# Twelve ident-by-xnT products at the head of TensorE's expert tile loop, each behind a wait on a scatter count

## The chip, the cores and the metric

The kernel runs on one core of a Trainium2 chip. The metric is the device time in microseconds (us) of one execution; lower is better. Three runs of the kernel before gave 1662.21, 1662.52 and 1665.05 us.

## What is computed

A chain of eight layers over an input `x` of 2048 tokens by 128 features, all in float32, each added to `x` (`x = x + layer(layernorm(x))`): a Mamba layer, a first mixture of experts, a linear attention, a second (gated) mixture of experts, then attention, experts, attention and a feed-forward layer. The change touches the function that computes the two mixtures of experts. In the reference they are:

```
# first: 8 experts, the best two of each token, 128 -> 512 -> 128
def body(acc, p):
    w1e, b1e, w2e, b2e, ce = p
    h = jax.nn.relu(xf @ w1e + b1e)
    y = h @ w2e + b2e
    return (acc + y * ce[:, None], None)
# second: the same with a gate
    h = jax.nn.silu(xf @ wg) * (xf @ wu)
    acc = acc + w[:, None] * (h @ wd)
```

`ce` and `w` are zero for all but a token's two best experts.

## The kernel before, in words

`program` calls one function per layer; `experts` is called twice, for `moe0` (not gated) and `moe1` (gated). Every function writes its work in one or more `nc.Block()` groups. In a block each engine has a list of its own: TensorE (PE), VectorE (DVE), ScalarE (ACT), GpSimd (POOL) and SyncE (SP, which only starts DMAs). Inside a block the engines meet only through semaphores that the code names.

`experts` computes only the pairs of token and expert that are chosen, in tiles of 128 rows (P = 128). It has two blocks:

- **The routing block** (line 903). The engines normalise `x` (16 tiles of 128 tokens, T = 16, in C = 4 chunks of CW = 512 tokens), turn it into `xnT`, compute the router's logits, pick two experts per token, and count for every pair a slot in a DRAM table `slots`, where each expert has a region of its own. POOL then sends the rows there: line 921 starts 2T = 32 indirect DMAs of 128 rows each, the **scatters**, and each adds 16 to the semaphore `s_sent` when it has landed. In `moe0` PE and DVE also add the second bias, beside the first scatters (lines 960 to 1060).
- **The tile block** (line 1087). NT = 2T + E - 1 = 39 tiles are computed one after the other (E = 8). SP waits until `s_sent` is 16 x 32, reads the first row of 13 tiles from the table `basei` (line 1083, a register load), and loads tile after tile from `slots` into 12 buffers `xg` (line 1095). PE reads the experts of 13 tiles from `whoi` (line 1083 too) and then runs a pipeline with four steps per tile: `turn_x` transposes the tile (line 1121), `hidden` multiplies by the expert's first matrix (line 1128; in `moe1` by a second one too, line 1131), `turn_h` transposes the result (line 1138), `down` multiplies by the last matrix (line 1147). DVE and ACT take the results out of the PSUM banks (lines 1175, 1192, 1199, 1202, 1208), and POOL sends the tile's answers out with an indirect DMA (line 1111). The register loads of PE and SP come again before tiles 13 and 26.

The weights `wa`, `wu`, `ba`, `wd` are loaded by DMAs of the routing block; their semaphore is `s_w`. `bank[7]` is a PSUM bank that `turn_h` uses for tiles of odd number. `k.ident` is a 128x128 identity and `k.xnT` the turned input, both float32.

The lines that the change and the prediction touch stand in TensorE's list of the tile block:

```
                pe.wait_ge(s_w, 16 * len(weights))
                for i in range(-2, NT + 1):
                    if 0 <= i + 2 < NT:
                        if (i + 2) % GROUP == 0:
                            experts_of.update(enumerate(values(ENGINE.PE, whoi, i + 2, E - 1), i + 2))
                        turn_x(i + 2)
```

Of the kernel before, what the change touches and what calls it, by code (L numbers as in the profile page):

```python
# [34 lines left out]
CW = CT * P  # L35
# [6 lines left out]
class Core:  # L42
# [64 lines left out]
    def sem(self, name):  # L107
        handle = self.nc.alloc_semaphore(name=name)
        self.part_sems.append(handle)
        return handle  # L110
# [726 lines left out]
def experts(k, name, gated):  # L837


    nc, t, C, T, E = k.nc, k.t, k.C, k.T, k.E  # L840
    L0, bank, pre = k.L, k.bank, name
# [2 lines left out]
    ROW = k.ROW  # L844
    NT = 2 * T + E - 1
    NB, NY, GROUP = 12, 6, 13
    slots, answers = k.slots[name], k.answers[name]
    tmp = ExitStack()
    sb = lambda n, shape, dt=F32: k.sb(f"{name}_{n}", shape, dt, tmp)
    sem = lambda n: k.sem(f"{name}_{n}")  # L850
    with tmp:
# [37 lines left out]
        s_w, s_v, s_rank, s_rows, s_same, s_slot, s_table, s_sent = (  # L889
            sem(n) for n in ("weights", "routing", "rank", "rows", "same_rows", "slot", "table", "sent"))  # L890
# [12 lines left out]
        with nc.Block() as block:  # L903
            @block.sync
            def _(sp):
                for dst, src in gates:
                    sp.dma_start(dst, src).then_inc(g_w, 16)
                for dst, src in weights:
                    sp.dma_start(dst, src).then_inc(s_w, 16)
# [158 lines left out]
        def wait(engine, sem, count):  # L1068

            if count > 0:  # L1070
                engine.wait_ge(sem, count)

        def loaded(engine, i):
            engine.wait_ge(s_ld[i % NB], 16 * (i // NB + 1))
# [5 lines left out]
        def values(engine, table, i, top_value):  # L1080

            reason = "counted up to the number of tiles, and the expert is held below their number"
            return nc.values_load_multi_w_load_instructions(
                table[0:1, i:min(i + GROUP, NT)], engines=[engine], min_val=0, max_val=top_value,
                skip_runtime_bounds_check_because=reason)[1]

        with nc.Block() as block:
# [26 lines left out]
            @block.tensor  # L1114
            def _(pe):
                experts_of = {}

                def turn_x(i):
                    loaded(pe, i)
                    wait(pe, s_xT, i)  # L1120
                    nc.tensor.transpose(bank[0][:, 0:P], xg[:, i % NB, 0:P], k.ident[:]).then_inc(s_tx, 1)  # L1121

                def hidden(i):
                    pe.wait_ge(s_xT, i + 1)
                    wait(pe, s_sg if gated else s_hh, i - 1)
                    one = bass.ds(experts_of[i], 1)
                    flat = lambda w: w[:, one, :].rearrange("p o f -> p (o f)")
                    nc.tensor.matmul(bank[1 + i % 2][:], xgT[:, i % 2, :], flat(wa), start=True, stop=True).then_inc(s_g, 1)  # L1128
                    if gated:
                        wait(pe, s_hh, i - 1)  # L1130
                        nc.tensor.matmul(bank[3 + i % 2][:], xgT[:, i % 2, :], flat(wu), start=True, stop=True)\
                            .then_inc(s_u, 1)

                def turn_h(i):
                    pe.wait_ge(s_hh, i + 1)
                    wait(pe, s_hT, i - 1)
                    for f in range(FB):
                        last = nc.tensor.transpose(bank[5 + 2 * (i % 2)][:, f * P:(f + 1) * P],  # L1138
                                                   h[:, i % 2, f * P:(f + 1) * P], k.ident[:])
                    last.then_inc(s_th, 1)  # L1140

                def down(i):
                    pe.wait_ge(s_hT, i + 1)
                    wait(pe, s_yw, i)
                    one = bass.ds(experts_of[i], 1)
                    for f in range(FB):
                        last = nc.tensor.matmul(bank[6][:, 0:P], hT[:, i % 2, f, :],  # L1147
                                                wd[:, one, f, :].rearrange("p o d -> p (o d)"),
                                                start=(f == 0), stop=(f == FB - 1))
                    last.then_inc(s_y, 1)  # L1150

                pe.wait_ge(s_w, 16 * len(weights))
                for i in range(-2, NT + 1):
                    if 0 <= i + 2 < NT:
                        if (i + 2) % GROUP == 0:
                            experts_of.update(enumerate(values(ENGINE.PE, whoi, i + 2, E - 1), i + 2))
                        turn_x(i + 2)
                    if 0 <= i + 1 < NT:
                        hidden(i + 1)
                    if 0 <= i < NT:  # L1160
                        turn_h(i)
                    if 0 <= i - 1:
                        down(i - 1)
# [1410 lines left out]
def program(nc, t, out, parts=PARTS):  # L2574
    with ExitStack() as ctx:
        k = Core(nc, ctx, t)
        for part in parts:
            if part == "mamba":
                mamba(k)
            elif part in ("moe0", "moe1"):  # L2580
                experts(k, part, gated=(part == "moe1"))
            elif part == "linear":
                linear(k)
            elif part in ("decay", "window"):
                softmax_mixer(k, part, windowed=(part == "window"))
            elif part == "deep":
                deep(k)
            elif part == "ffn3":
                ffn3(k)
            k.end_part()  # L2590
        store(k, out)
# [64 lines left out]
```

## Time and profile before

| what | value |
|---|---|
| three runs | 1662.21, 1662.52, 1665.05 us |
| the profiled execution | 1660.62 us |
| its span (first to last instruction) | 1658.8 us |
| mean granted TensorE clock, as a share of full speed | 0.864 |
| PE busy | 1204.5 us (73%) |
| DVE busy | 875.2 us (53%) |
| ACT busy | 651.1 us (39%) |
| POOL busy | 532.7 us (32%) |
| scatters (line 921) | 64, from 447.3 us to 732.3 us |

The profiled execution took 1660.62 us, 1.8 us more than its span; the sums of the prediction are made against it. The tile block of `moe0` lies at about 490 to 600 us of the span, that of `moe1` at about 736 to 880 us. A float32 matmul of 512 columns leaves two MATMUL records in the trace. The granted clock stands at 0.50 or 1.00, 1.2 or 2.4 GHz. "PEq", "SPq" and so on are an engine's sequencer: semaphores, branches, register loads, DMA issues.

### The profile page before, as it was taken

To read this page: it belongs to the slowest core of one execution; us is meant where nothing else is said; L and a number is where in the kernel's file an instruction comes from. 1 tells how busy PE (TensorE), PEld (TensorE's weight loads), DVE (VectorE), ACT (ScalarE), POOL (GpSimd) and SP (SyncE) were. 2 spreads that over 40 slices of the span, in tenths; PEclk is the share of its full clock that TensorE was granted. 3 is DMA by queue.
4 is the path that set the end of the run, shared out by engine and by line. 5 is a ranking of instruction groups with operands and counts; after the bars stand their busy time and mean duration, and the time that the engine had idled before them with its cause. 6 is when DMAs were issued, how large, how long until landed. Compare 5 with 4: busy or idle time off the path is not lost. (4 is left out here: it accounts for less than half of the span.)

```text
span 1658.8 us, 23925 instructions
## 1 busy us (share of the span) xinstructions
PE 1204.5 (73%) x8267; PEld 723.8 (44%) x8267; DVE 875.2 (53%) x2052; ACT 651.1 (39%) x1106; POOL 532.7 (32%) x661
## 2 busy tenths in 40 slices
PE   6605776768339948219991799988982799969998
PEld 3201222225327735206660577763331567744544
DVE  3407999995515452503336688854653667651010
ACT  2605555553102210103330677745652676632131
POOL 6107765662253320352234322202007544300000
PEclk9858999999559975559995799998995999979999
DMA  2993000000411120511102000001000000020000
GB/s 64 189 188 60 1 0 1 0 0 1 162 55 53 48 69 1 167 56 36 42 28 67 2 2 2 3 2 39 1 1 8 1 3 2 2 72 1 0 0 25
DMA packets 88024, 60.26 MB, mean 36 GB/s; under 512 B 15346, under 2 KB 78724, under 8 KB 87780
## 3 DMA queue, kind: packets, MB, share of 16 engines
q1 hardware_dynamic: 83364, 49.38, 14.0%
q0 software_dynamic: 4544, 9.38, 1.7%
q8 instruction: 68, 1.11, 0.3%
q14 instruction: 48, 0.39, 0.1%
HBM read 30.21 MB, written 28.52 MB: 35 GB/s over the span
## 5 line engine op out<-in xcount | busy, mean ns | idle before, releaser
L809 POOL TENSOR_TENSOR hC<-h,Cs 128x1024 f32<-128x1024 f32 x64 | 153.3, 2395 | 137.4 <-DVE h L738 137.1
L599 PE MATMUL bank<-hC,ident 128*128 128x512 f32 x256 | 129.2, 628 | 43.8 <-POOL hC L809 43.7
L738 DVE TENSOR_TENSOR_SCAN h<-bank,state,dBx 128x512 f32<-128x512 f32 x128 | 157.2, 1270 | 2.2 <-ACT bank L674 0.2
L1111 POOL DMA_INDIRECT moe_answers<-moe_yw,moe_xg x78 | 74.7, 958 | 173.6 <-DVE moe_yw L1208 173.6
L2057 DVE TENSOR_REDUCE window_mx<-bank 128x2 f32<-128x384 f32 x128 | 69.6, 556 | 76.1 <-PE bank L1912 75.0
L1175 ACT ACTIVATE moe_hT<-bank 128x512 f32<-128x512 f32 x78 | 46.6, 597 | 154.8 <-PE bank L1138 154.8
L727 DVE TENSOR_TENSOR dBx<-dtx,bank 128x1024 f32<-128x1024 f32 x64 | 76.6, 1196 | 49.0 <-PE bank L586 49.0
L2057 DVE TENSOR_REDUCE decay_mx<-bank 128x2 f32<-128x512 f32 x128 | 85.1, 685 | 25.0 <-PE bank L1912 24.8
L674 ACT ACTIVATE bank<-dt,A 128x512 f32<-128x512 f32 x128 | 83.2, 682 | 37.9 <-DVE h L738 37.9
L2027 ACT ACTIVATE decay_pb<-bank 128x512 f32<-128x512 f32 x128 | 75.6, 596 | 48.0 <-PE bank L1925 45.5
L599 PEld LDWEIGHTS bank<-hC,ident 128*128 128x128 f32 x256 | 44.4, 192 | 106.7 <-POOL hC L809 71.1
L586 PE MATMUL bank<-BC,sel 128*128 128x512 bf16 x64 | 25.5, 398 | 87.4 <-PEq L258 57.6
L178 ACT ACTIVATE xnT<-bank 128x512 f32<-128x512 f32 x24 | 14.3, 597 | 179.6 <-PE bank L169 179.6
L1147 PE MATMUL bank<-moe_wd,moe_hT 128*128 x624 | 83.1, 276 | 1.9 <-DVE moe_yw L1208 1.9
L1128 PE MATMUL bank<-moe_wa,moe_xgT 128*128 x156 | 84.4, 623 | 0.0
L1121 PE MATMUL bank<-ident,moe_xg 128*128 128x128 f32 x78 | 22.5, 288 | 82.5 <-DMA moe_xg<-moe_slots 74.6
L921 POOL DMA_INDIRECT moe_slots<-moe_rows,moe_slot x64 | 61.7, 963 | 59.8 <-DVE moe_slot L1014 40.9
L158 POOL TENSOR_TENSOR rstd<-veps,mhalf 128x4 f32<-128x4 f32 (+1 forms) x14 | 23.3, 1664 | 172.3 <-DVE veps L140 172.0
L1147 PEld LDWEIGHTS bank<-moe_wd,moe_hT 128*128 128x128 f32 x624 | 76.3, 193 | 2.6 <-issue 2.6
L2027 ACT ACTIVATE window_pb<-bank 128x384 f32<-128x384 f32 x128 | 61.6, 487 | 40.0 <-PE bank L1925 39.7
L680 ACT ACTIVATE Cs<-bank 128x512 f32<-128x512 f32 x64 | 38.2, 596 | 73.7 <-POOL hC L809 65.3
L169 PE MATMUL bank<-ident,xn 128*128 128x128 f32 x64 | 17.2, 424 | 68.3 <-DVE xn L149 68.3
(452 smaller groups left out, 2912.9 us busy)
## 6 DMA issues: line engine op xcount, KB each, us to landing
moe_slots<-blank SPq DMA_DIRECT2D x16, 1040.0 KB, 17.9
moe_xg<-moe_slots SPq DMA_DIRECT2D x78, 65.0 KB, 1.8
moe_wa<-in_moe_w SPq DMA_DIRECT2D x2, 2048.0 KB, 9.3
moe_back<-moe_answers SPq DMA_DIRECT2D x16, 256.0 KB, 4.8
moe_ba<-in_moe_b SPq DMA_DIRECT2D x1, 2048.0 KB, 14.2
moe_wu<-in_moe_wu SPq DMA_DIRECT2D x1, 2048.0 KB, 14.3
deep_w<-in_deep_w SPq DMA_DIRECT2D x3, 512.0 KB, 5.0
moe_answers<-moe_yw,moe_xg POOLq DMA_INDIRECT x78, 2.2
```

Source lines behind the costliest of these rows:

```text
L599: last = nc.tensor.matmul(sum_bank(hh)[:], k.ident[:], hC[:, u % 2, hh, :], start=(n == 0), stop=(n == NS - 1))
L674: nc.scalar.activation(decay_bank(u, hh)[:], dt[:, hh, cols(c)], ACT.Exp, scale=A[:, hh, n:n + 1]).then_inc(q_dA, 1)
L727: v.tensor_tensor(dBx[:, u % 2], dtx[:, :, cols(c)], b_bank[:, None, :].to_broadcast([P, H, CW]), ALU.mult).then_inc(q_dBx, 1)
L738: v.tensor_tensor_scan(h[:, u % 2, hh, :], decay_bank(u, hh)[:], dBx[:, u % 2, hh, :], state[:, n, hh:hh + 1], ALU.mult, ALU.add).then_inc ...
L809: g.tensor_tensor(hC[:, u % 2], h[:, u % 2], Cs[:, u % 2, None, :].to_broadcast([P, H, CW]), ALU.mult).then_inc(q_hC, 1)
L921: nc.gpsimd.indirect_dma_start(slots, bass.IndirectOffsetOnAxis(index, 0), rows[j][:, i, :], None)\
L1111: nc.gpsimd.indirect_dma_start(answers, bass.IndirectOffsetOnAxis(index, 0), yw[:, i % NY, :], None)\
L1128: nc.tensor.matmul(bank[1 + i % 2][:], xgT[:, i % 2, :], flat(wa), start=True, stop=True).then_inc(s_g, 1)
L1147: last = nc.tensor.matmul(bank[6][:, 0:P], hT[:, i % 2, f, :], wd[:, one, f, :].rearrange("p o d -> p (o d)"), start=(f == 0), stop=(f == ...
L1175: nc.scalar.activation(hT[:, i % 2].rearrange("p f q -> p (f q)"), bank[5 + 2 * (i % 2)][:], ACT.Copy if gated else ACT.Relu).then_inc(s_h ...
L2027: nc.scalar.activation(pb[:, w % 4, :], bank[2 + w % 2][:, 0:2 * HW], ACT.Exp).then_inc(s_ex, 1)
L2057: nc.vector.tensor_reduce(mx[:, 2 * g:2 * g + 2], bank[g % 2][:, 0:2 * HW].rearrange("p (j q) -> p j q", j=2), AX.X, ALU.max, negate=True) ...
```

## The change

At the head of TensorE's list in the tile block, behind the wait for the weights and ahead of the first register load, a loop of twelve steps is added. Each step waits until `s_sent` has reached the count of 20, 21, ... 31 scatters, and then makes one product of `ident` with the first 512 columns of `xnT` into `bank[7]`. Nothing reads the result.

```
@@ experts @@
     NB, NY, GROUP = 12, 6, 13
+    BUSY = 12
     slots, answers = k.slots[name], k.answers[name]
@@ tile block, TensorE @@
                 pe.wait_ge(s_w, 16 * len(weights))
+                for sent in range(2 * T - BUSY, 2 * T):
+                    pe.wait_ge(s_sent, 16 * sent)
+                    nc.tensor.matmul(bank[7][:], k.ident[:], k.xnT[:, 0:CW], start=True, stop=True)
                 for i in range(-2, NT + 1):
```

Below stand TensorE's instructions in program order around the border of the two blocks of `moe0`. Line numbers of the changed kernel are one higher up to the loop and four higher behind it. Semaphores are named in such rows by the first that held their number: `m_sel` is `s_sent` here, `w_in` is `s_w`, `m_rstd` the load of the first tile; the barrier is named in full. Before:

```order
L967 MATMUL bank<-moe_bd,moe_combT 128x128 x3
L903 UNCONDITIONAL_BRANCH
L1114 UNCONDITIONAL_BRANCH [waits barrier_Pool_Activation_PE_DVE_SP_release]
L1083 TENSOR_LOAD moe_whoi [waits w_in]
L1121 MATMUL bank<-ident,moe_xg 128x128 [waits m_rstd]
L1121 MATMUL bank<-ident,moe_xg 128x128 [waits m_dt_relu,m_xn]
```

And in the changed kernel:

```order
L968 MATMUL bank<-moe_bd,moe_combT 128x128 x3
L904 UNCONDITIONAL_BRANCH
L1115 UNCONDITIONAL_BRANCH [waits barrier_Pool_Activation_PE_DVE_SP_release]
L1156 MATMUL bank<-xnT,ident 128x512 [waits m_sel,w_in]
L1156 MATMUL bank<-xnT,ident 128x512 [waits m_sel] x11
L1084 TENSOR_LOAD moe_whoi
L1122 MATMUL bank<-ident,moe_xg 128x128 [waits m_rstd]
```

The twelve products stand between the branch into the tile block and the register load; `moe1` has the same rows. The list of POOL, in the changed kernel, at the same border:

```order
L158 TENSOR_TENSOR rstd<-veps,mhalf 128x12 [waits ln_ve]
L922 DMA moe_slots<-moe_rows,moe_slot 17408x130 [waits c_ident,c_more,c_zeroed,filled]
L922 DMA moe_slots<-moe_rows,moe_slot 17408x130 x31
L904 UNCONDITIONAL_BRANCH
L1107 UNCONDITIONAL_BRANCH [waits barrier_Pool_Activation_PE_DVE_SP_gather]
```

All 32 scatters stand ahead of POOL's branch at the block's end, as before; POOL gathers the barrier that releases the other engines. No instruction of POOL, DVE, ACT or SP has moved.

## Rows read from the trace of the kernel before

**Rows 1.** The page: busy time of each engine, its share, instructions.
```profile
PE 1204.5 (73%) x8267; PEld 723.8 (44%) x8267; DVE 875.2 (53%) x2052; ACT 651.1 (39%) x1106; POOL 532.7 (32%) x661
```
**Rows 2.** Waits of TensorE, 430 to 500 and 680 to 745: total, times, longest.
```profile
PE bank L1121 <- DMA moe_xg<-moe_slots: 25.6, 1, 25.6
...
PE bank L1121 <- DMA moe_xg<-moe_slots: 49.0, 1, 49.0
```
**Rows 3.** Instructions of line 921: ns min/median/max, first and last start; time to landing.
```profile
L921 POOL DMA_INDIRECT moe_slots<-moe_rows,moe_slot x64: 954/958/1220, 447.3 to 732.3; - x64
...
DMA to landing us min/median/max: 2.3/2.3/3.4
```
**Rows 4.** Sequencer instructions of line 903, the routing block's end, same columns.
```profile
L903 POOLq EVENT_SEMAPHORE  x4: 17/17/17, 490.4 to 736.1; - x4
...
L903 PEldq DRAIN  x2: 575/1336/2098, 466.4 to 689.8; - x2
...
L903 POOLq DRAIN  x2: 17805/17815/17825, 472.5 to 718.1; - x2
...
L903 PEldq EVENT_SEMAPHORE  x2: 51/51/51, 490.5 to 736.1; - x2
```
**Rows 5.** PE's register loads of line 1083, 485 to 500 and 730 to 745.
```profile
L1083 PEldq TENSOR_LOAD <-moe_whoi x1: 1307/1307/1307, 490.6 to 490.6; - x1
...
L1083 PEldq TENSOR_LOAD <-moe_whoi x1: 1096/1096/1096, 736.3 to 736.3; - x1
```
**Rows 6.** Timeline, both tile blocks' first instructions: start, us, engine, line.
```profile
494.00 0.48 PE L1121 MATMUL bank<-ident,moe_xg 128*128 128x128 f32 x1 [25.57 <-DMA moe_xg<-moe_slots]
...
739.41 0.47 PE L1121 MATMUL bank<-ident,moe_xg 128*128 128x128 f32 x1 [49.05 <-DMA moe_xg<-moe_slots]
...
740.67 1.95 PE L1128 MATMUL bank<-moe_wa,moe_xgT 128*128 x2
742.41 1.92 PE L1131 MATMUL bank<-moe_wu,moe_xgT 128*128 x2
...
747.01 1.02 PE L1128 MATMUL bank<-moe_wa,moe_xgT 128*128 x2
747.87 0.59 PE L1131 MATMUL bank<-moe_wu,moe_xgT 128*128 x1
```
**Rows 7.** Windows: stretch, length, busy of PE, PEld, DVE, ACT, POOL, granted clock, DMA, GB/s.
```profile
494.00:499.40 5.40, 4.92 (x10) 2.35 (x11) 1.66 (x5) 0.00 (x0) 0.00 (x0) 0.50 0.50 120
499.40:505.00 5.60, 5.60 (x36) 4.15 (x35) 3.34 (x8) 1.79 (x3) 0.96 (x1) 1.00 0.06 18
739.40:745.15 5.75, 5.20 (x8) 2.28 (x9) 1.37 (x4) 0.60 (x1) 0.00 (x0) 0.50 0.51 121
...
1494.80:1499.50 4.70, 4.70 (x6) 2.12 (x7) 0.53 (x1) 1.97 (x2) 0.00 (x0) 0.50 0.00 0
```
**Rows 8.** Instructions of line 599, whose operands have the added product's shape and type.
```profile
L599 PE MATMUL bank<-hC,ident x256: 590/592/1223, 138.8 to 381.6; 128*128 128x512 f32 x128
```
**Rows 9.** PE's register load before tile 26 of `moe0`, and the timeline beside it.
```profile
L1083 PEldq TENSOR_LOAD <-moe_whoi x1: 3210/3210/3210, 553.9 to 553.9; - x1
...
554.04 1.06 PE L1147 MATMUL bank<-moe_wd,moe_hT 128*128 x8
...
557.28 0.33 PE L1121 MATMUL bank<-ident,moe_xg 128*128 128x128 f32 x1 [2.18 <-issue]
```
**Rows 10.** Windows, same columns: behind that load, and after the last tile of `moe0`.
```profile
557.40:560.80 3.40, 3.40 (x10) 2.15 (x10) 0.98 (x2) 0.33 (x1) 0.00 (x0) 0.50 0.14 34
...
595.00:598.40 3.40, 0.07 (x1) 0.00 (x0) 0.35 (x1) 0.00 (x0) 0.96 (x1) 1.00 0.13 41
598.40:600.00 1.60, 0.00 (x0) 0.00 (x0) 0.00 (x0) 0.00 (x0) 0.00 (x0) 0.50 0.31 84
```
**Rows 11.** Windows, same columns: a long stretch of the tile block of `moe1`.
```profile
747.00:860.00 113.00, 110.36 (x589) 74.63 (x588) 43.28 (x105) 41.81 (x70) 32.58 (x34) 1.00 0.13 36
```
**Rows 12.** Instructions of line 586, 512 columns in bf16, one record each.
```profile
L586 PE MATMUL bank<-BC,sel x64: 379/389/609, 131.8 to 371.7; 128*128 128x512 bf16 x64
```

More of the change, by code:

```diff
@@ L846, in experts @@
     NB, NY, GROUP = 12, 6, 13
+    BUSY = 12
     slots, answers = k.slots[name], k.answers[name]
@@ L1152, in _ @@
                 pe.wait_ge(s_w, 16 * len(weights))
+                for sent in range(2 * T - BUSY, 2 * T):
+                    pe.wait_ge(s_sent, 16 * sent)
+                    nc.tensor.matmul(bank[7][:], k.ident[:], k.xnT[:, 0:CW], start=True, stop=True)
                 for i in range(-2, NT + 1):
```

## The prediction

> **What bounds the kernel now.** The page comes first: TensorE is the busiest engine, with 73% of the span [rows 1]. A share over eight layers says little of one place, so the reading goes to the place that is edited. The waits of TensorE around it come next: two are long, 25.6 and 49.0 us, both of line 1121, and both end with a load from the slot table [rows 2]. They are the time in which POOL starts the scatters. So at the head of each tile block TensorE has nothing to do until the first tile has come; behind that it is the bound: in `moe1` it is busy for 110.36 of 113.00 us [rows 11]. Whatever holds TensorE beyond the arrival of the first tile moves the whole tile block, and with it everything behind it, by as much.
>
> The windows show the second fact. When the first tile comes (494.0 and 739.4 us), the granted clock is 0.50, the lower of its levels; it stays there for 5.40 and 5.75 us and is 1.00 afterwards [rows 7]. In these stretches TensorE is busy for 4.92 and 5.20 us. At twice the clock this work takes half as long, so a TensorE that is at 2.4 GHz when the first tile arrives saves at most 2.46 + 2.60 = 5.1 us in the two parts. That is all that there is to be gained.
>
> The third view decides: what stands between the scatters and TensorE's list of the tile block. The new products are in the tile block, the scatters in the routing block. The program order shows a barrier there that POOL gathers and that releases the others. In the trace, TensorE's drain at the end of the routing block starts at 466.4 and 689.8 us, long before the scatters are out, but its semaphore instruction behind it comes only at 490.5 and 736.1 us [rows 4]. POOL's own drain starts at 472.5 and 718.1 us and takes 17.8 us: it ends at 490.3 and 735.9 us, and POOL's semaphore instructions follow at 490.4 and 736.1. The last scatter starts at 732.3 us and lands 2.3 us later by the median, 3.4 at most [rows 3]: at 734.6 to 735.7 us, before the barrier opens. **So TensorE can't be beside a scatter with anything that stands in the tile block.** When it gets there, all 32 have landed, the twelve waits on `s_sent` hold nothing back, and the twelve products run in one piece.
>
> **The change part by part.** Removed: nothing. Moved: TensorE's first register load, from the head of the block to behind the products. Added in each of the two parts: twelve waits and twelve float32 products of 512 columns.
>
> *The waits.* 0 us, since their counts are reached. If they weren't, they would be the thing wanted.
>
> *The products, start.* Before, the register load of TensorE is its first instruction in the block and starts at 490.6 and 736.3 us [rows 5]. The products take that place. With about 0.2 us to the first of them, they start at 490.8 and 736.5 us.
>
> *The products, length.* At the low clock two products of this size follow each other 742.41 - 740.67 = 1.74 us apart, at the high one 747.87 - 747.01 = 0.86 us [rows 6]. Those have another stationary operand than the identity; the one group with the identity and 512 float32 columns has 592 ns for a record, as have theirs, and 1223 at most [rows 8]. I take the clock to rise after as long a stretch as it did for the work that now starts here, 5.40 and 5.75 us [rows 7]. In `moe0` 5.40 / 1.74 = 3.1 products are slow and 8.9 fast: 5.40 + 8.9 x 0.86 = 13.1 us. In `moe1` 5.75 / 1.74 = 3.3 are slow: 5.75 + 8.7 x 0.86 = 13.2 us. They end at 503.9 and 749.7 us.
>
> *The delay.* The first tile's transpose started at 494.00 and 739.41 us [rows 6]; now it starts at 503.9 and 749.7. That is 9.9 + 10.3 = 20.2 us later, on the engine that bounds the block. The loads of SP aren't delayed: twelve tiles lie ready.
>
> *The clock.* TensorE comes to the first tile at the high clock and gets back the 2.46 + 2.60 = 5.1 us from above.
>
> *The register load.* It took 1.3 and 1.1 us at this place [rows 5] and is now behind the products. I cost it at nothing, and its cover is the products: before tile 26 the same load starts at 553.9 us, when the last eight records of line 1147 are only about to run (554.04, for 1.06 us) [rows 9]. So TensorE's sequencer runs ahead of its array by at least sixteen instructions with their weight loads, four of the new products and 3.4 us of time, more than either load. If it doesn't, the load adds 1.3 + 1.1 = 2.4 us, and if it takes the 3.2 us that it took there, 6.4 us.
>
> *What moves with the tile block.* The stalls of the later register loads fall at other moments. After the one before tile 26 the clock was low for 3.40 us [rows 10], which cost half of it, 1.7 us; after the other three it wasn't. With another phase it can be none of four, or two: -1.7 to +1.7 us. I take 0.
>
> The sum is 20.2 - 5.1 = **+15.1 us** against the profiled execution: a span of 1658.8 + 15.1 = 1673.9 us and a time of 1660.62 + 15.1 = 1675.7 us. The median of the three runs is 1.9 us above the profiled execution. The prediction is for the median: 1662.5 + 15.1 = **1677.6 us**, 0.9% slower.
>
> *A rule against the row.* Two neighbouring products of this shape stand 1.74 us apart at the low clock and 0.86 at the high one [rows 6]. The Trainium skill, in "TensorE: Matmul & The Clock Gate", section "Back-to-back issue gap", gives the gap as the number of columns over 1.2 GHz cold and over 2.4 GHz warm plus 2.5 ns, and makes no difference by type; by it twelve products would take 12 x 0.427 = 5.1 us, the end would be at 495.9 and 741.6, and the sum 4.1 - 5.1 = -1 us. The rows have four times that distance for float32, and I follow them.
>
> **The rivals.**
>
> *The products cost what bf16 products cost.* The nearest row is line 586, 512 columns in bf16, one record of 389 ns by the median and 609 at most [rows 12]. Twelve would be done in at most 12 x 0.61 = 7.3 us, at 498.1 and 743.8 us: 4.1 + 4.4 - 5.1 = +3.4 us, 1666 us. Against it: operand types are float32 in the diff, and line 599 with the same types has two records of 592 ns each. 2%.
>
> *It works as it is worded, and the kernel gets faster.* If TensorE entered the tile block while POOL was still at its scatters, the products would be spread over the last twelve, the last behind the 31st landing, at about 733.4 us. Even at 0.86 us it ends before the first tile arrives at 739.41. Nothing is late, and the gain is up to 5.1 us: 1657.4 us. It decides at one point: the first product must start before 736.1 us (490.5 in `moe0`). For it speaks only the semaphore that the loop waits for; against it TensorE's semaphore instruction at 490.5 and 736.1 behind a drain that was over at 468.5 and 690.4 [rows 4]. And then the gap of some 5 us to the first tile would count: after the last tile of `moe0` the clock is down 3.4 us into the idle time [rows 10], so that the first tile would find 1.2 GHz again and the time would be 1662.5. The same page of the Trainium skill, section "HAM oscillation — how this bites in real kernels", says this of bursts with waits for data between them, which speaks against the change even where it does what it says. 3% for both: 1% faster, 2% no change.
>
> *The register load isn't covered.* +2.4 to +6.4 us on top of the sum, 1680 to 1684 us. 10%.
>
> *The clock rises sooner or later.* If it rose at once, the twelve would take 12 x 0.86 = 10.3 us; if it never did, 12 x 1.74 = 20.9 us, and the 5.1 us would be lost too. The second isn't credible for a TensorE without a pause. Three starts lie between 4.70 and 5.75 us [rows 7], the first of them the last layer's, where TensorE is as dense as with the new products. 4.70 gives 12.7 us for the products. I allow twice the spread of the three, 2 us sooner or later, which is 1 us per part: -2 to +2 us. This is the width of the forecast and not a case of its own.
>
> **How the numbers follow.** Forecast 85%, load uncovered 10%, bf16 price 2%, as worded 3%. The range takes in the forecast's own width (2 us for the clock and 1.7 for the phases on each side: 1673.9 to 1681.3), a us below it for the start of the products, and the nearer end of the uncovered load: **1673 to 1682.5 us**. What lies outside are the two small rivals and the farther end of the load. A measurement of this kernel can tell about 0.2%, 3.3 us, from no change; the bf16 price, +3.4, sits on that bound and is counted within it. Faster 1%, within it 4%, slower 95%.
>
> **What would show it.** Right: in the changed kernel twelve products (24 records) of the new line in one piece from about 490.8 and 736.5 us, none before 490.5 or 736.1; the first three or so 1.7 us apart, the rest 0.86; the first transpose of line 1122 at 503 to 505 and 749 to 751 us, with no wait for a DMA, and at clock 1.00; TensorE's register load inside the stretch of the products; POOL's scatters and drain unchanged; every later layer's start some 15 us later. Wrong: products between 472 and 490 us, or spaced 1.26 us like the scatters; an idle TensorE of over 1 us between the last product and the first transpose; products of 0.4 us.

## The result and the profile after

| | before | changed |
|---|---|---|
| runs | 1662.12, 1662.21, 1662.52, 1665.05 us | 1672.54, 1674.94, 1675.11, 1675.12 us |
| median | 1662.37 us | 1675.03 us |
| profiled execution / span | 1660.62 / 1658.8 us | 1672.54 / 1670.7 us |

The changed kernel is slower: the ratio is 1.0069 with a 95% interval of 1.0051 to 1.0086, +12.7 us between the medians. The forecast was +15.1 us and 1677.6 us in a range of 1673 to 1682.5. On another chip, later in the study, the same two kernels stood at 1.0096 (1.0079 to 1.0112), +15.5 us between the medians.

The page, and the new line's instructions (ns min/median/max, first and last start), in the changed kernel:

```profile
span 1670.7 us, 24015 instructions
PE 1225.2 (73%) x8307; PEld 733.1 (44%) x8315; DVE 875.4 (52%) x2052; ACT 651.1 (39%) x1106; POOL 531.6 (32%) x661
...
L1156 PE MATMUL bank<-xnT,ident x48: 592/592/1193, 492.1 to 756.9; 128*128 128x512 f32 x48
```

TensorE has 20.7 us more busy time [rows 1], and its weight loads 9.3 us; VectorE, ScalarE and GpSimd are within 1.1 us of before. The 48 records are two for each of 24 products, none of them before 492.1 us. (Weight loads rose by 48, matmul records only by 40: eight matmul records are missing from this trace.)

The sequencers at the end of the routing block (line 904 now), and TensorE's first register load, same columns:

```profile
L904 PEldq DRAIN  x2: 573/1336/2100, 467.7 to 697.6; - x2
L904 POOLq DRAIN  x2: 17799/17823/17847, 473.8 to 725.9; - x2
...
L904 PEldq EVENT_SEMAPHORE  x2: 51/51/51, 491.9 to 743.8; - x2
...
L1084 PEldq TENSOR_LOAD <-moe_whoi x1: 1316/1316/1316, 497.3 to 497.3; - x1
```

As before [rows 4], TensorE drains early and is released at 491.9 and 743.8 us, when POOL's drain is over (473.8 + 17.8 = 491.6). The register load runs from 497.3 to 498.6 us, while the products run.

The timeline of TensorE (start, us, engine, line) at both tile blocks:

```profile
492.12 13.08 PE L1156 MATMUL bank<-xnT,ident 128*128 128x512 f32 x24 [22.36 <-PEq L904]
505.04 0.27 PE L1122 MATMUL bank<-ident,moe_xg 128*128 128x128 f32 x1
...
508.53 1.06 PE L1129 MATMUL bank<-moe_wa,moe_xgT 128*128 x2
...
744.10 13.38 PE L1156 MATMUL bank<-xnT,ident 128*128 128x512 f32 x24 [46.02 <-PEq L904]
757.32 0.27 PE L1122 MATMUL bank<-ident,moe_xg 128*128 128x128 f32 x1
...
762.45 1.02 PE L1129 MATMUL bank<-moe_wa,moe_xgT 128*128 x2
```

The twelve lie in one piece, 0.2 and 0.3 us behind the release, and the first transpose follows without a wait, where it had waited for a DMA [rows 6]. Windows (stretch, length, busy of PE, PEld, DVE, ACT, POOL, granted clock, DMA, GB/s):

```profile
492.10:497.20 5.10, 5.08 (x6) 2.18 (x7) 0.00 (x0) 0.00 (x0) 0.00 (x0) 0.50 0.31 73
497.20:505.00 7.80, 7.80 (x19) 3.37 (x18) 0.00 (x0) 0.00 (x0) 0.00 (x0) 1.00 0.22 56
744.10:749.80 5.70, 5.70 (x7) 2.49 (x8) 0.00 (x0) 1.10 (x1) 0.00 (x0) 0.50 0.31 73
749.80:757.30 7.50, 7.50 (x18) 3.18 (x17) 0.00 (x0) 0.00 (x0) 0.00 (x0) 1.00 0.21 53
```

So the slow stretch now holds three products and not the first tile [rows 7]; the first tile comes at 2.4 GHz.

A yardstick for the rest: from TensorE's release at the barrier to its first product of the third tile (line 1128), where the pipeline runs evenly. It holds the delay and the clock of one part and nothing of the other layers.

| kernel | `moe0`, us | `moe1`, us |
|---|---|---|
| before, first chip | 499.67 - 490.5 = 9.2 | 747.01 - 736.1 = 10.9 |
| changed | 508.53 - 491.9 = 16.6 | 762.45 - 743.8 = 18.7 |

Together +15.2 us, against a forecast of 15.1. The span grew by 11.9 only. Where each step now starts later: the release in `moe0` 1.4 us, its third tile 8.9, the load of its answers (line 1101) 10.5, the last products of the linear attention (line 1378) 7.7, the release in `moe1` 7.7, its third tile 15.4, the first product of the attention behind it (line 1871) 15.5, of the third expert layer (line 1503) 14.0, of the last layer (line 2496) 12.3, and the final store 11.9. The two steps of the change are in that ladder (+7.4 and +7.8, to the rounding); the other steps are 1.4 us lost ahead of them, 1.6 lost behind the third tile of `moe0`, and 2.8, 1.5 and 1.7 won in three later layers.

### The profile page after: what moved, and what is told of

It is laid out like the page before. It is cut to its first block and busy times, and to the rows that moved or that the text cites. A ratio compares the mean times of both kernels' runs of the same rounds, so it can differ in the third digit from the quotient of the medians.

```text
span 1670.7 us, 24015 instructions
## 1 busy us (share of the span) xinstructions
PE 1225.2 (73%) x8307; PEld 733.1 (44%) x8315; DVE 875.4 (52%) x2052; ACT 651.1 (39%) x1106; POOL 531.6 (32%) x661
## 5 line engine op out<-in xcount | busy, mean ns | idle before, releaser
L2061 DVE TENSOR_REDUCE decay_mx<-bank 128x2 f32<-128x512 f32 x128 | 85.2, 685 | 23.6 <-PE bank L1916 23.2
L1156 PE MATMUL bank<-xnT,ident 128*128 128x512 f32 x48 | 26.5, 718 | 68.4 <-PEq L904 68.4
L1196 DVE COPY moe_xgT<-bank 128x128 f32<-128x128 f32 x78 | 22.0, 283 | 95.7 <-PE bank L1122 95.4
```

The source lines that it names most:

```text
L2061: nc.vector.tensor_reduce(mx[:, 2 * g:2 * g + 2], bank[g % 2][:, 0:2 * HW].rearrange("p (j q) -> p j q", j=2), AX.X, ALU.max, negate=True) ...
```

## The experiments

They ran on three other chips (experiments 1 to 4 on one, 5, 7, 8 and the first run of 6 on the next, the rest on the last), so each is compared with the kernel before on its own chip (median 1656 to 1659 us there) by its ratio, and by the yardstick. No kernel leaves out a part of the computation; they differ in products that nothing reads. Twelve were run.

**1. The products without their waits.**

```
-                for sent in range(2 * T - BUSY, 2 * T):
-                    pe.wait_ge(s_sent, 16 * sent)
+                for _ in range(12):
```

> The changed kernel without its twelve waits on the scatter count; the twelve products stay at the head of the tile block. Theory (the barrier between the blocks holds TensorE until all scatters have landed, so the waits hold nothing back): same as the changed kernel, 1675 +- 1.5 us, first product 0.2 us behind TensorE's semaphore instruction at the barrier, products 13.1 and 13.4 us long. Rival (the waits themselves delay TensorE, or pace the products): at least 3 us faster than the changed kernel, with the products closer together.

Measured: ratio 1.0073 (1.0050 to 1.0096), as the changed kernel. Products 0.15 and 0.1 us behind the release, 13.49 and 12.47 us long; yardstick 17.0 and 17.7 us. The waits hold nothing back.

**2. The waits without the products.**

```
                 for sent in range(2 * T - BUSY, 2 * T):
                     pe.wait_ge(s_sent, 16 * sent)
-                    nc.tensor.matmul(bank[7][:], k.ident[:], k.xnT[:, 0:CW], start=True, stop=True)
```

> The changed kernel without its twelve products; the twelve waits stay. Theory (all of the loss is the time of the products): same as the kernel before, 1662.4 +- 1.5 us, first transposes 3.5 and 3.3 us behind the barrier as before. Rival (waits cost): each wait of some tenths of a us ahead of the register load makes the first transpose late, 1664 us and above.

Measured: 0.9996 (0.9983 to 1.0010). First transposes 3.3 and 3.2 us behind the release, yardstick 8.3 and 10.9 us. The waits cost nothing; all of the loss is the products.

**3. The products moved into the routing block.** The wait for `s_bx` is in `moe0` alone, where the bias adds read bank 7; `s_side` holds one semaphore for each of the scatters 20 to 31, which counts in place of `s_sent`.

```
                         last.then_inc(s_bo, 1)
+                    pe.wait_ge(s_bx, C)
+                for s in s_side:
+                    pe.wait_ge(s, 16)
+                    nc.tensor.matmul(bank[7][:], k.ident[:], k.xnT[:, 0:CW], start=True, stop=True)
@@ tile block, SyncE @@
-                sp.wait_ge(s_sent, 16 * 2 * T)
+                sp.wait_ge(s_sent, 16 * (2 * T - BUSY))
+                for s in s_side:
+                    sp.wait_ge(s, 16)
```

> The twelve products moved to the end of TensorE's list in the routing block, each behind a semaphore of its own of one of the scatters 20 to 31 (none at the head of the tile block). Theory (only there can they be beside scatters): the products lie between about 472 and 490 us, nothing is late, and nothing is added to the path. The clock rises about 5 us into them; whether it is still high at the first tile, 4 to 5 us after the last product, decides the gain: if it has fallen again 1662.4 us, if it holds until 494.0 and 739.4 us 1658 us (4.4 us less). I expect it to have fallen, 1662.4 +- 1.5 us. Rival (the place does not matter, the products cost their time wherever they stand): 1670 us and above.

Measured: 1.0082 (1.0064 to 1.0099), a miss for the whole. The two parts differ. TensorE in `moe1`, timeline:

```profile
732.23 8.60 PE L976 MATMUL bank<-xnT,ident 128*128 128x512 f32 x14 [29.37 <-DMA moe_slots<-moe_rows,moe_slot]
741.13 3.38 PE L976 MATMUL bank<-xnT,ident 128*128 128x512 f32 x6 [0.31 <-DMA moe_slots<-moe_rows,moe_slot]
744.77 2.29 PE L976 MATMUL bank<-xnT,ident 128*128 128x512 f32 x4 [0.26 <-DMA moe_slots<-moe_rows,moe_slot]
752.43 0.48 PE L1130 MATMUL bank<-ident,moe_xg 128*128 128x128 f32 x1 [5.38 <-DMA moe_xg<-moe_slots]
```

Here they do lie beside the scatters, paced by them once the clock is high, and the last ends at 747.1 us, 1.6 us before the release at 748.7. But the windows behind them:

```profile
747.00:750.60 3.60, 0.06 (x1) 0.00 (x0) 0.00 (x0) 1.28 (x1) 0.00 (x0) 1.00 0.00 0
750.60:757.40 6.80, 4.42 (x8) 1.99 (x9) 0.59 (x3) 0.60 (x1) 0.00 (x0) 0.50 0.48 110
```

The clock falls at 750.6 us, 3.5 us into the idle time, and the first tile meets 1.2 GHz again: yardstick 759.65 - 748.7 = 11.0 us, nothing gained. That is the "works as it is worded" rival in its case of no gain. In `moe0` the timelines of DVE and PE say:

```profile
489.79 0.69 DVE L1064 TENSOR_TENSOR X<-bank,X 128x512 f32<-128x512 f32 x1 [11.98 <-remote]
490.54 12.56 PE L976 MATMUL bank<-xnT,ident 128*128 128x512 f32 x24 [10.60 <-DVE X L1064]
```

VectorE's last bias add came late, the products waited for it because of bank 7, and their 12.6 us stood ahead of the barrier, which opened at 503.3 us. POOL's drain was over at 487.7 us, so the products held the barrier; the whole lost 12.5 us by the medians. The wait for the bank that I had added is the loss.

**4. The same with three more products at the head of the tile block.** The lines below are added to experiment 3.

```
                 pe.wait_ge(s_w, 16 * len(weights))
+                for _ in range(3):
+                    nc.tensor.matmul(bank[7][:], k.ident[:], k.xnT[:, 0:CW], start=True, stop=True)
```

> As the kernel with the products in the routing block, and three more of them at the head of the tile block, where TensorE waits some 3.3 us for its first tile. Theory: the clock is high from the first twelve when TensorE passes the barrier 1.5 us after the last, so the three take 0.86 us each, 2.6 us, end before the first tile arrives, and keep the clock high: first transposes 3.3 to 3.6 us behind the barrier as before, at clock 1.00, and 2 x 2.2 us gained: 1658 +- 1.5 us. Rival (the clock falls in the pause at the barrier): three slow products, 5.2 us, first transposes 2 us late, 1662 to 1665 us.

Measured: 1.0067 (1.0042 to 1.0093); `moe0` loses as above (release at 501.4 us). In `moe1`, the timeline:

```profile
743.22 2.81 PE L1163 MATMUL bank<-xnT,ident 128*128 128x512 f32 x6 [1.94 <-PEq L905]
746.82 0.33 PE L1130 MATMUL bank<-ident,moe_xg 128*128 128x128 f32 x1 [0.79 <-DMA moe_xg<-moe_slots]
...
752.00 1.02 PE L1137 MATMUL bank<-moe_wa,moe_xgT 128*128 x2
```

Three fast products fit into the wait for the first tile and keep the clock up. Yardstick 752.00 - 743.1 = 8.9 us, 2.0 below the 10.9 of the kernel before. First transposes come 3.7 us behind the release, in place of 3.3: SyncE's twelve more waits stand ahead of its first load.

**5. Six products beside earlier scatters, in bank 0, and three at the head.** SyncE's waits for the semaphores stand in the routing block now. The lines below are those of the routing block that differ from experiment 4, without the moved waits and the choice of the scatters 24 to 29; the three products at the head go to bank 0 too.

```
-    BUSY = 12
+    BUSY, SKIP = 6, 24
-                    pe.wait_ge(s_bx, C)
-                    nc.tensor.matmul(bank[7][:], k.ident[:], k.xnT[:, 0:CW], start=True, stop=True)
+                    nc.tensor.matmul(bank[0][:], k.ident[:], k.xnT[:, 0:CW], start=True, stop=True)
```

> Six products in the routing block, into bank 0, each behind a semaphore of its own of one of the scatters 24 to 29, with no wait for the bias adds; three more at the head of the tile block; SyncE waits for the six semaphores in the routing block, ahead of the barrier. Theory: the six lie beside scatters and end before POOL's drain, so the barrier is not late; the clock is high there; the three take 2.6 us of the 3.3 us in which TensorE waits for its first tile; first transposes 3.3 to 3.5 us behind the barrier, at clock 1.00, and 2.2 to 2.6 us gained per part: 4 to 5 us faster than the kernel before, ratio 0.9970 to 0.9985. Rival (the first tiles are not bound by TensorE's clock, or the six hold the barrier): ratio 1.000 or above.

Measured: 1.0003 (0.9992 to 1.0014), another miss. Timeline and windows of `moe1`:

```profile
723.75 8.20 PE L977 MATMUL bank<-xnT,ident 128*128 128x512 f32 x12 [34.18 <-DMA moe_slots<-moe_rows,moe_slot]
735.46 4.51 PE L1162 MATMUL bank<-xnT,ident 128*128 128x512 f32 x6 [3.52 <-PEq L905]
```

```profile
735.40:736.20 0.80, 0.74 (x2) 0.49 (x3) 0.00 (x0) 0.78 (x1) 0.00 (x0) 1.00 0.00 0
736.20:739.60 3.40, 3.40 (x5) 1.23 (x4) 0.00 (x0) 0.51 (x1) 0.00 (x0) 0.50 0.27 65
```

The six end at 732.0 us; TensorE then idles for 3.5 us, and the clock falls at 736.2, in the middle of the three, which take 4.5 us in place of 2.6. In `moe0` it falls at 487.0, 2.8 us after the last of the six. Yardstick 8.0 and 9.5 us: better than before, but the whole shows none of it. Why is open. In this profile the first scatter of `moe0` starts at 445.1 us, 1.9 to 3.4 us later than in the three others of that chip and ahead of all added products, and the tile block of `moe0` has two stretches at the low clock where those of experiments 6 and 7 have one; whether the other runs share this is not shown.

**6. Only two products at the head.** Run twice, on two chips.

```
-                for sent in range(2 * T - BUSY, 2 * T):
-                    pe.wait_ge(s_sent, 16 * sent)
+                for _ in range(2):
```

> Only two products at the head of the tile block, without waits. Theory (up to the arrival of the first tile TensorE is free, and the clock rises some 5 us after TensorE starts, whatever it starts with): both at the low clock, 3.5 us, first transposes 3.6 to 3.8 us behind the barrier in place of 3.3 to 3.5; the clock rises 1.5 to 2 us into the tiles in place of 5.4; 1.0 to 1.5 us gained per part: ratio 0.998 to 0.999. Rival (every product costs its time): 3.5 us per part lost, ratio 1.004.

> The kernel with two products at the head of the tile block again, beside the others. Theory: ratio to the kernel before 0.9975 to 0.9995, first transposes 3.6 us behind the barrier. Rival (the first reading was chance): ratio 0.9995 to 1.001.

Measured: 0.9983 (0.9968 to 0.9999) and 0.9979 (0.9965 to 0.9992): faster than the kernel before, in the first run only just clear of no change. Timeline of `moe1` in the first:

```profile
730.57 3.75 PE L1155 MATMUL bank<-xnT,ident 128*128 128x512 f32 x4 [45.98 <-PEq L904]
734.11 0.42 PE L1122 MATMUL bank<-ident,moe_xg 128*128 128x128 f32 x1
...
739.84 1.02 PE L1129 MATMUL bank<-moe_wa,moe_xgT 128*128 x2
```

Two slow products end 3.6 us behind the release, 0.3 us past the arrival of the tile. Yardstick 7.3 and 9.3 us, in the second run 7.3 and 9.5. The edit is the changed kernel's with another number, and has the other sign.

**7. Twelve products in bfloat16.** The lines below are added to the kernel before.

```
+                for _ in range(12):
+                    nc.tensor.matmul(bank[7][:].rearrange("p (a q) -> p a q", a=4), k.identb[:],
+                                     k.onesb[:, None, :].to_broadcast([P, 4, P]), start=True, stop=True)
```

> Twelve products of 512 columns in bfloat16 (a bfloat16 identity with a constant of ones) in place of the float32 ones, at the head of the tile block, without waits. Theory (a float32 product costs four times a bfloat16 one, and that price is the loss): 0.43 us each at the low clock, 5.1 us in all, first transposes 5.3 us behind the barrier, 2 us late, with the clock high at or soon after them: ratio 0.9985 to 1.001. Rival A (the count of products sets the price, not their type): as the changed kernel, ratio 1.007. Rival B (such products do not raise the clock): first transposes 2 us late and slow, ratio 1.0025.

Measured: 0.9990 (0.9978 to 1.0001). Timeline of `moe1`:

```profile
732.39 5.28 PE L1155 MATMUL bank<-onesb,identb 128*128 128x512 bf16 x12 [45.95 <-PEq L904]
737.46 0.37 PE L1122 MATMUL bank<-ident,moe_xg 128*128 128x128 f32 x1
```

Twelve take 5.1 us up to the transpose (5.0 in `moe0`), 0.42 each; the float32 ones take 13. Yardstick 8.6 and 10.4 us. The clock rises 4.9 and 5.3 us after the first of them, as it does with the others.

**8. Twenty-four products.**

```
-                for _ in range(12):
+                for _ in range(24):
```

> Twenty-four float32 products at the head of the tile block, without waits. Theory (all products behind the barrier are on the path, and behind the rise of the clock each costs 0.86 us): first transposes 23.5 us behind the barrier, 12 x 0.86 = 10.3 us per part above the changed kernel, ratio to the kernel before 1.0195 +- 0.0015. Rival (a fixed cost of the new loop, or a queue that fills): less than 15 us above the changed kernel in all, or more than 25.

Measured: 1.0238 (1.0213 to 1.0263), +39 us where 32 were expected: a miss by the whole. Timeline of `moe1`:

```profile
751.58 23.63 PE L1155 MATMUL bank<-xnT,ident 128*128 128x512 f32 x48 [45.94 <-PEq L904]
775.05 0.27 PE L1122 MATMUL bank<-ident,moe_xg 128*128 128x128 f32 x1
```

First transposes 22.9 and 23.6 us behind the release; yardstick 26.4 and 28.7 us, 9.8 and 10.0 us above the changed kernel where 10.3 were expected. So 19.8 us of the difference to the changed kernel are priced, and the price of a product is as forecast. The expectation for the whole started from the changed kernel's 1.0069; from the 1.0096 of experiment 9, 20.6 us more would be 1.0220, within the interval. Against the trace of the kernel before in experiment 9 (another chip) the final store is 38.1 us later: 35.9 us by the two yardsticks, 1.5 more behind the third tile of `moe0`, 2.9 in the attention behind `moe1`, and 2.2 less elsewhere.

**9. The changed kernel and the kernel before again, on one chip.** No edit.

> The changed kernel again, on the same chip as the others. Theory: ratio to the kernel before 1.006 to 1.009, products at the barrier and not beside the scatters in both parts, also where the routing block of the first part ends by VectorE and not by POOL. Rival: on another chip the products are not in one piece.

> The kernel before, one look. On the second and third chip VectorE's last bias add of the first part started 15 to 17 us late, after the last scatter, in every kernel, and set the barrier. If that belongs to the chip or the run and not to the products, it stands here too: the bias add (line 1057) after POOL's last scatter, the barrier 0.5 us behind it. If the edits caused it, the bias adds end at 20 us before the barrier as in the first profile of the kernel before.

Measured: 1.0096 (1.0079 to 1.0112) for the changed kernel, a little above what was expected; products in one piece behind the release in both parts, 12.48 and 13.07 us long; yardstick in `moe1` 759.08 - 740.8 = 18.3 us. The kernel before shows 495.71 - 487.0 = 8.7 and 743.19 - 732.7 = 10.5 us. With 502.04 - 486.0 = 16.0 us in `moe0` of the changed kernel the parts give 7.3 + 7.8 = 15.1 us, the medians 15.5. The kernel before shows VectorE's late bias add too, here with POOL's last scatter:

```profile
486.13 0.69 DVE L1057 TENSOR_TENSOR X<-bank,X 128x512 f32<-128x512 f32 x1 [16.18 <-remote]
...
482.52 0.96 POOL L921 DMA_INDIRECT moe_slots<-moe_rows,moe_slot  x1 [0.30 <-issue]
```

No edit of the study causes it.

**10. What the runs point to.** In `moe1` twelve products beside the scatters 20 to 31 and three at the head; in `moe0`, where VectorE's end is uncertain, two at the head and none beside the scatters. SyncE's waits stand ahead of the barrier. The lines below differ from experiment 4; the moved waits are not shown.

```
-    BUSY = 12
+    BUSY = 12 if gated else 0
-                    pe.wait_ge(s_bx, C)
-                for _ in range(3):
+                for _ in range(3 if gated else 2):
```

> In the gated part: twelve products in the routing block, one behind each of the scatters 20 to 31, and three at the head of the tile block, with SyncE's waits for the twelve semaphores ahead of the barrier. In the first part: only two products at the head of the tile block. Theory: in the gated part the last of the twelve ends within 2 us of the barrier, the clock is high over the barrier and the three, first transposes 3.3 us behind the barrier at clock 1.00, 2.6 us gained; in the first part 1 to 1.5 us gained as with two products alone: ratio 0.9973 to 0.9985. Rival (the twelve hold the barrier of the gated part by over 1 us, or the clock falls): ratio 0.999 or above.

Measured: 0.9967 (0.9953 to 0.9981), a little below what was expected, 4.7 us below the kernel before by the medians and the fastest of the study. Timeline of `moe1`:

```profile
719.17 8.78 PE L977 MATMUL bank<-xnT,ident 128*128 128x512 f32 x14 [29.25 <-DMA moe_slots<-moe_rows,moe_slot]
729.08 4.95 PE L977 MATMUL bank<-xnT,ident 128*128 128x512 f32 x10 [1.14 <-DMA moe_slots<-moe_rows,moe_slot]
735.77 2.81 PE L1162 MATMUL bank<-xnT,ident 128*128 128x512 f32 x6 [1.74 <-PEq L905]
739.01 0.33 PE L1129 MATMUL bank<-ident,moe_xg 128*128 128x128 f32 x1 [0.42 <-DMA moe_xg<-moe_slots]
...
744.27 1.02 PE L1136 MATMUL bank<-moe_wa,moe_xgT 128*128 x2
```

TensorE pauses for 1.7 us at the barrier, the clock stays up, and the first transposes are 3.3 us behind the release, as without products. Yardstick 498.63 - 491.3 = 7.3 and 744.27 - 735.7 = 8.6 us, where the kernel before has 8.7 and 10.5 on this chip: 3.3 us by the parts, 4.7 by the medians, whose interval (3.1 to 7.8 us) takes in both.

## Why the prediction was right

**The barrier, right.** Products start 0.2 to 0.3 us behind the release in both parts, and with the waits away nothing changes (experiment 1); with the products away the loss is gone (2). Moved ahead of the barrier they do lie beside the scatters (3, 10), so it was the place and not the wait that decided.

**The length of the products, right.** Forecast 13.1 and 13.2 us, measured 13.08 and 13.38. The clock rose after 5.1 and 5.7 us; 5.40 and 5.75 had been taken.

**The price by type, right.** The rule of one gap for all types, from the Trainium skill, "TensorE: Matmul & The Clock Gate", section "Back-to-back issue gap", fits the bfloat16 products of experiment 7 (5.0 and 5.1 us for twelve; 12 x 0.427 = 5.1) and not the float32 ones, which take 12.3 to 13.3 us up to the transpose in the three traces with twelve of them. With its price the change would have been the 0.9990 of experiment 7.

**The delay, right.** Forecast 9.9 + 10.3; measured from release to first transpose, 13.14 - 3.5 = 9.6 and 13.5 - 3.3 = 10.2 us. The times of day named for `moe1` (products from 736.5 us, transpose at 749 to 751) were wrong, for they leave out that the delay in `moe0` moves `moe1` too: 744.1 and 757.3 us. The sum does not use them.

**What the clock gives back, a little too large.** Forecast 2.46 + 2.60 as a bound. From first transpose to third tile it was 5.67 us and is 3.49 in `moe0`, 7.60 and 5.13 in `moe1`: 2.2 + 2.5. Not all of that stretch scales with TensorE's clock: the 0.47 us for which TensorE waits for VectorE behind the first transpose of `moe0` are there at either clock. Delay and give-back are each 0.4 us below the forecast and cancel, so that 15.2 us for 15.1 is partly luck.

**The register load, right.** It runs beneath the products at 497.3 us.

**"What moves with the tile block. I take 0": the term that was mis-sized.** The span grew by 11.9 us and the two parts by 15.2, so all else makes -3.3 us in the profiled execution: 1.4 us lost ahead of every added product, and -4.7 us behind them. I had allowed 1.7 us either way, for the stalls of the register loads in `moe0` and `moe1`. There the term was +1.6 us, from two stretches at the low clock in `moe0`'s tile block where one had been [rows 10]; windows of the changed kernel, same columns:

```profile
535.00:538.20 3.20, 3.20 (x15) 3.01 (x14) 1.03 (x3) 0.60 (x1) 0.00 (x0) 0.50 0.11 26
569.00:572.20 3.20, 3.20 (x15) 3.05 (x14) 1.15 (x3) 0.60 (x1) 0.00 (x0) 0.50 0.11 26
```

What I left out is that every later start of TensorE has such a term. The linear attention won 2.8 us: 1.2 since its clock rose 3.0 us after TensorE's start and not 5.5, and 1.6 since it then stayed up until 640.6 us of the span, for 10.2 us and not 6.8. Two later layers won 1.5 and 1.7. The second pair of traces (experiment 9) shows what of this comes again. There the changed kernel is 1.0 us earlier at the release in `moe0`, 8.1 later at the release in `moe1` and 15.7 later at the final store: all else behind the products makes +1.6 us in place of -4.7. The linear attention wins nothing there (+0.1), and the stretch up to the last layer loses 1.3 where it won 1.7. But the +1.6 us in `moe0`'s tile block and the gain in the attention behind `moe1` (1.5 us, there 1.8) stand in both pairs, so these may belong to the change; no run holds all else fixed. The +12.7 us of the first chip fall short of the forecast by such steps, the +15.5 of the last do not.

**The upper end of the range, loosely set.** The width gives 1681.3 us, and the nearer end of the uncovered load 1677.6 + 2.4 = 1680; 1682.5 follows from neither. The result, 1675.03, lies in the range with either.

**The rivals.** "As worded" was right in its second half: beside the scatters, and still no gain, since the clock falls before the first tile (experiment 3, `moe1`). Uncovered load: no. bf16 price: no.

## What to carry to other kernels

Filler work belongs in the program section whose idle time it is to fill: a wait on a counter does not carry it past a barrier, and the release of that barrier in the trace tells how much idle time is left behind it. Here 3.3 to 3.5 us were left; two products of 1.74 us gain 0.2%, twelve lose 0.7 to 1.0%. To keep TensorE's clock up until data comes, the filler has to reach up to it: the clock outlived pauses of 1.7 and 1.9 us, and with longer ones it fell 2.8 to 5.1 us after the last product, and then most of the first filler was in vain. And such a product must not wait for a bank that another engine may read late.

## What was not expected of the hardware

- The clock can fall 2.8 us after TensorE's last product (487.0 us in `moe0` of experiment 5), and 3.5 and 4.2 us after it at other places of experiments 3 and 5. In `moe0` of experiment 3 it outlived an idle time of 3.9 us and fell at 508.2 us, 1.2 us after the first transpose had begun and 5.1 us after the last product. The moment is no fixed distance.
- On the three later chips VectorE waited with no engine named while POOL started scatters back to back: 6 to 17 us for the last two bias adds of `moe0` (one operand in PSUM, one in SBUF), the last of them only after POOL's last scatter, in the kernel before too. The copies of `moe_combT` between them, with their one operand in PSUM, waited too (2.8 us in the kernel before of experiment 9, 8.3 in experiment 4), so it is not the pair of operands that makes the difference. On the first chip none was late. What held them was not found.
- A shift of some us in one layer is given back or added in other layers, by up to 3 us each, through the moments at which the clock rises and falls. Two kernels within 0.2% of each other can't be told apart by one profile; the stretch between two fixed points around the edit can.
